# Spreading the weight statistics of a transformer layer: from one burst per attention head to pairs after each query tile, and into the output projection

## The reference

```python
x = x + attn(layernorm(x), Wq, bq, Wk, bk, Wv, bv, Wo, bo)   # causal, 16 heads of 128, rope
x = x + ffn(layernorm(x), w_gate, w_up, w_down)

def _weight_quant(w):
    scale = jnp.clip(jnp.mean(jnp.abs(w)), EPS, None)        # one number per matrix
    return jnp.clip(jnp.round(w / scale), -1.0, 1.0) * scale
def _bitlinear(x, w):
    return jnp.einsum('...i,oi->...o', _act_quant(x), _weight_quant(w))
# ffn: bitlinear(silu(bitlinear(x, w_gate)) * bitlinear(x, w_up), w_down)
```

## Time and profile before

| what | us |
|---|---|
| median of 13 runs (10388.69 to 10520.22) | 10472.44 |
| the profiled execution | 10480.55 |
| its span on the slowest core, core 4 | 10478.8 |
| spans of the eight cores | 10417.0 to 10478.8 |
| PE busy in the span | 6001.0 (57%) |
| DVE busy in the span | 4629.9 (44%) |
| ACT busy in the span | 1869.8 (18%) |
| POOL busy in the span | 1367.7 (13%) |

### The profile page before, as it was taken

How to read it: one execution, slowest core, us unless ns; L and a number is a source line. 1 busy time by engine, 2 the same in 40 slices (tenths; PEclk the granted TensorE clock), 3 DMA queues, 4 the chain that set the end, 5 groups by cost and what they waited for, 6 DMA issues and landing times.

```text
span 10478.8 us, 90777 instructions; the slowest of 8 cores (10417.0 to 10478.8 us)
## 1 busy us (share of the span) xinstructions
PE 6001.0 (57%) x23243; PEld 2279.6 (22%) x23698; DVE 4629.9 (44%) x5216; ACT 1869.8 (18%) x3294; POOL 1367.7 (13%) x770
## 2 busy tenths in 40 slices
PE   0007466596464545546455078788878826384847
PEld 0002222242010111101012033333333312232323
DVE  6403233223434334343436467777777642414140
ACT  3531011002232333323221000000000010101010
POOL 0002122000000000000000133333333200000000
PEclk9999799797676676767678589999999957686767
DMA  2482321331313132221344433343333213343323
GB/s 93 157 271 55 74 49 41 80 79 44 116 63 119 62 103 78 88 93 66 106 125 142 144 128 122 128 128 125 125 126 125 97 59 136 111 143 107 134 95 123
DMA packets 637659, 1115.47 MB, mean 106 GB/s; under 512 B 339954, under 2 KB 421874, under 8 KB 567282
## 3 DMA queue, kind: packets, MB, share of 16 engines
q1 hardware_dynamic: 433380, 530.71, 17.1%
q10 hardware_dynamic: 158976, 302.06, 8.3%
q0 software_dynamic: 44816, 276.88, 8.3%
HBM read 874.62 MB, written 218.10 MB: 104 GB/s over the span
## 4 chain that ended last, share of the span: by engine, by line
DVE 34%; PE 30%; DMA 10%; issue 7%; ACT 7%; POOL 5%; SPq 3%; ACTq 2%; DVEq 1%; another core or an unknown queue 1%; POOLq 0%
PE pb L68 23%; DVE p_cu L68 5%; PE p2S L68 3%; SPq L68 3%; DVE p_hqt L68 3%; DVE t_w L68 3%; DVE wa_tmp L68 2%; POOL p_wdtb L68 2%; DVE p_pm L68 2%; DVE p_wf L68 2%; ACTq L68 2%; ACT p_E L68 2%; DVE p_invr L68 2%; DMA wa_t<-wgT 2%; DMA wa_t<-wuT 2%
## 5 line engine op out<-in xcount | busy, mean ns | idle before, releaser
L68 PE MATMUL pb<-p_wgt,p_xiT 128*128 128x512 bf16 x4015 | 1073.1, 425 | 801.6 <-DVE p_ht L68 430.2
L68 PE MATMUL pb<-p_wds,p_hTg 128*128 128x512 bf16 x4009 | 1022.8, 422 | 104.8 <-DMA p_wds<-wdtd 88.5
L68 ACT ACTIVATE p_E<-pb,p_negB 128x512 bf16<-128x512 f32 x1280 | 879.4, 687 | 633.7 <-PE pb L68 452.4
L68 DVE TENSOR_TENSOR p_cu<-g_sxinv,p4a_swn 128x1 f32<-128x1 f32 x256 | 754.3, 2947 | 28.2 <-DVE p_cg L68 2.1
L68 PEld LDWEIGHTS pb<-p_wgt,p_xiT 128*128 128x128 bf16 x4096 | 426.9, 107 | 1431.0 <-issue 1072.5
L68 PE MATMUL p2S<-p_E,g_ones_colb 128*1 128x512 bf16 x1280 | 539.7, 422 | 308.4 <-DVE p_invr L68 307.0
L68 PE MATMUL pb<-k_pp_xT,k_pp_W 128*128 128x512 bf16 x2007 | 465.1, 383 | 299.7 <-ACT k_pp_qb L68 196.2
L68 PE MATMUL pb<-p_dump,g_ones_colb 128*1 128x512 bf16 x192 | 107.2, 593 | 910.5 <-DVE p_dump L68 791.5
L68 DVE TENSOR_REDUCE wa_tmp<-wa_t 128x1 f32<-128x2048 f32 x192 | 438.9, 2286 | 354.4 <-DMA wa_t<-wgT 120.0
L68 PEld LDWEIGHTS pb<-p_wds,p_hTg 128*128 128x128 bf16 x4096 | 433.4, 106 | 690.5 <-issue 501.6
L68 PE MATMUL pb<-p_qT,p_kT 128*128 128x512 bf16 x1263 | 551.5, 440 | 51.9 <-ACT p_E L68 38.9
(11 more groups left out here) (168 smaller groups left out, 6853.6 us busy)
## 6 DMA issues: line engine op xcount, KB each, us to landing
wa_t<-wgT POOLq DMA_DIRECT2D x64, 1024.0 KB, 5.9
wa_t<-wuT POOLq DMA_DIRECT2D x64, 1024.0 KB, 5.8
wa_t<-wdT POOLq DMA_DIRECT2D x64, 1024.0 KB, 5.4
p_wf<-wdT SPq DMA_DIRECT2D x64, 1024.0 KB, 5.9
p_wf<-wgT SPq DMA_DIRECT2D x64, 1024.0 KB, 5.8
p_wf<-wuT SPq DMA_DIRECT2D x64, 1024.0 KB, 5.3
hfpd<-p_ht ACTq DMA_DIRECT2D x256, 256.0 KB, 2.9
p_wds<-wdtd SPq DMA_DIRECT2D x64, 1024.0 KB, 6.5
```

The costliest lines, as they stand in the source:

```text
L68: real = getattr(eng, meth)(*a, **k)
```

## The change

The feed moves inside the loop over query tiles, with 2 chunks after each of the four tiles, in place of 12 after each head. That places 8 per head, 128 in attention. The other 64 go into the loop over row blocks of the output projection, 4 behind each block. The epilogue moves behind that loop.

```diff
@@ attention, loop over t @@
                 eitems.extend(mk_epi(h, t, t % 2))
+                wa_feed(2)
             hrel[sl] = (sT, sT.v)
-            wa_feed(12)
@@ output projection, ahead of the loop over tb @@
             wsem.inc(G.dma_start(dst3, rows), 16)
 
-        wa_feed(len(wa_items))
-        wa_epilogue()
         cin = [dm["c0"], dm["c1"]]
@@ end of the loop over tb @@
             x1rel[sl] = [(x1sem[sl], x1sem[sl].v), (sS, sS.v), (sV, sV.v)]
+            wa_feed(4)
+        wa_feed(len(wa_items))
+        wa_epilogue()
         wait(V, (sV, sV.v), (sS, sS.v))
```

## The result

The changed kernel took 10143.81 us in the median of 11 runs, the kernel before 10480.57 us in the median of 48. The ratio is 0.9672 (95% interval 0.9644 to 0.9701): 3.3% faster, some 337 us; the fastest runs of the two, 10382.44 and 10043.36 us, lie 339 us apart. The forecast was 10170 us.

What follows compares the result with a forecast made beforehand. DVE's chunk burst at each head's end was taken to bound attention, DVE the output projection's pace. From 10480.55 us, -728 +165 +23 +230 +8 gave 10179, less 8 for the median 10170; range 10,060 to 10,330.

Steps and rivals of the forecast that it cites:

- The burst leaves the head's end: Attention, head ends: PE's wait for the squares falls to 9.4 us per head over 14 heads, gaining 639.6 us.
- The tail of heads 14 and 15: Attention, last two heads: reciprocal waits of 51.7 and 51.4 us become ordinary tile ends of 7.3, gaining 88.5 us.
- Pairs behind the first three tiles: Attention, 48 tile ends: the pair delays the reciprocal, PE's wait grows from 3.84 to 7.3 us, costing 165 us.
- a sign of being wrong: Attention: the prediction counts as wrong if tile ends cost more than 8 us.
- The clock behind a longer wait: Attention, tile ends: longer idle keeps PE's clock low for longer, 1.5 us per head, costing 23 us in all.
- The upper bound of 71 us: Attention: cost of the clock term if all 48 longer gaps paid at the lower clock level.
- Four chunks in each row block: Output projection: each block grows by 14.4 us to 31.2, costing 230 us over 16 blocks.
- the epilogue's 8: Behind the output projection's loop: nothing covers the moved epilogue any more, costing 8 us.
- Wo's wait: Start of the output projection: PE's wait for Wo stays; two chunk loads issued behind Wo's parts add 0.
- Transfers did not bound the output projection: Denies a rival: output projection bound by transfers, blocks of 39 us, 125 us more, 10,295 us; chance 0.12.
- The head's load: Rival, head ends: k usable only with v, PE idles 23.6 us, 199 us more, 10,370 us; chance 0.06.
- The slower case: Rival, attention: the clock stays down throughout, 770 us more, 10,920 us; chance 0.04.

Runs made afterwards that it cites:

- e7: e6 with three slots for q, k and v, so a head's loads are issued a whole head earlier; 9,676 us, ratio 0.9217 to the kernel before.
- e4: The changed kernel with the pairs of the first three tiles one step later, behind the next tile's first reciprocal; ratio 0.9576 to the kernel before.
- e1: The changed kernel without any chunks, neither their loads nor their sums, epilogue still behind the output projection's loop; ratio 0.9295 to the kernel before.
- e8: The changed kernel with four chunk tiles in place of two, so a row block's four chunks are loaded ahead; ratio 0.9538 to the kernel before.
- e6: The changed kernel with all 192 chunks as pairs inside attention's tiles, none at tile ends or row blocks; 9,772 us, ratio 0.9320 to the kernel before.

## Why the prediction was right

**The burst leaves the head's end.** Forecast: 639.6 us less waiting for the squares, 9.4 us left per head. Measured: 648 less (791.5 to 143.4). Of the 143.4, the first two waits take about 20, as before, which leaves 8.8 per head. What came next was named rightly, k's landing, and e7 shows it by moving it away. The tail of heads 14 and 15, forecast at 88.5, can't be told apart from the next term in the sum of waits; their longest wait fell from 51.7 to 8.3, 1 us over the forecast.

**Pairs behind the first three tiles.** Forecast: +165 for 48 of them and -88.5 for the last two heads, so +76.5 on the reciprocal's waits. Measured: +77. Two of these 64 waits take 8.3 us, over the 8 us that the prediction set as a sign of being wrong; they are the ends of heads 14 and 15, and the median is 7.1. e4 shows that it was the order on DVE, not the work: the same pair behind the reciprocal costs next to none of it.

**The clock behind a longer wait.** This term of 23 us was mis-sized, its mechanism was right. On core 4 the first matmul of `p2S` behind the reciprocal took 0.38 us at 16 of 63 tile ends before, and at none after; the others took 0.58 or so the earlier trace rows. But few further key blocks are slow for it: of the 1280 matmuls of `p2S`, 274 took over 0.5 us before, 289 after and 279 in e1. Ten to fifteen key blocks at 0.63 us more each (1.48 less 0.85) would be 6 to 9 us, an estimate. It fits e1's 1 to 8 us, and the 4 to 6 us by which attention on cores 4 to 7 shortened less than the waits named above. The rule of the Trainium skill (TensorE: Matmul & The Clock Gate, section "Why this matters for your kernels") on idle gaps, which the prediction weighed, holds in its direction, since every gap now ends at the lower level. The upper bound of 71 us wasn't reached.

**Four chunks in each row block.** Forecast 230 us with the epilogue's 8 beside it, measured 244 on core 4. By e1 and e8 a block's price is 11.3 us of series work and 3.6 of waiting for loads, 14.9 against the forecast 14.4. The epilogue itself ran from 5384.2 to 5392.3, its 8 us; in e1, where it stands at the same place without chunks, the stage is 6 us over that of before. Wo's wait stayed at some 59 us from issue to first matmul (60.7 before), although the two chunk loads issued behind Wo needed up to 61.8 us to land: they came behind, as assumed.

**The rivals.** Transfers did not bound the output projection: blocks of 30.5 to 33.2 us, not 39, and e8 gained by putting more loads in flight. The head's load cost k's landing and no more. The slower case is out: attention's granted clock rose.

**The sum.** Attention: forecast -540, measured -563 on core 4. Output projection with the epilogue: +238 and +244. Net -302 and -319, and most of what lies between is the clock term. By the medians over the cores it is -588 and +245, net -343, and medians of whole runs differ by 337. Core 4, on whose rows the forecast was made, had the shortest attention of the eight before.

## What to carry to other kernels

Background work on an in-order engine cost what it delayed, not what it lasted: in attention of this kernel all 192 chunks cost 18 us between key blocks in which DVE is idle and 761 in bursts, and 128 of them cost 174 at tile ends ahead of a reciprocal. When a burst goes, ask which load it had hidden, and give that load an earlier issue too. A place off the former critical path is no free place: where the engine itself sets the pace, each chunk cost its full length here, and part of its load as well with only two tiles.

## What the runs showed of the hardware that was not expected

In eight of the ten profiled executions pairs of neighbouring cores lost some 20 to 120 us in one stage or two, and not always the same: cores 4 and 5 in the down projection of the kernel before (2050 and 2030 us against 1919 to 1938) and cores 2 and 3 in its attention (3006 and 3007 against 2929 to 2953), cores 4 and 5 in attention of e4 (2269 and 2262 against 2189 to 2214) and of e6 (2243 and 2239 against 2197 to 2208). These stretches (core 0 and core 4 of the kernel before, same code, the down projection, then two parts of it on core 4; columns as above) show it as clock:

```profile
8529.00:10448.00 1919.00, 1045.79 (x5120) 503.04 (x5120) 631.78 (x720) 245.36 (x1088) 130.41 (x128) 0.74 0.36 123
```

```profile
8429.00:10478.00 2049.00, 1147.93 (x5033) 528.95 (x5120) 631.17 (x719) 245.23 (x1088) 128.65 (x128) 0.69 0.33 115
...
9260.00:9292.00 32.00, 31.73 (x120) 13.28 (x122) 0.00 (x0) 0.00 (x0) 0.00 (x0) 0.81 0.34 112
9292.00:9324.00 32.00, 31.82 (x124) 13.38 (x125) 0.00 (x0) 0.00 (x0) 0.00 (x0) 0.81 0.21 79
```

The mean granted clock is 0.74 in the one and 0.69 in the other, and PE is busy for 102 us more. The last two rows show why: PE works almost without a break there, and the granted clock stands at 0.81. The matmuls take 0.434 to 0.438 us in these 64 us, 0.379 on core 0 from 9270 to 9290, where the granted clock is 1.00. So a granted clock between 0.50 and 1.00 is not always a mix of the two levels in time, as it was read ahead of the prediction. Added up over the clock's records in the trace, core 4 stood at 0.81 for 648 of the 2050 us and core 6 for none of its 1933. The other stages named above have 386 to 673 us of it on the cores that lost time. It costs only where PE's pace counts: cores 4 and 5 of e1 had some 1500 us of it in gate and up, and that stage is as long there as on the other cores (2558 and 2559 us against 2560 to 2563).

The profiled executions of the changed kernel and of e8 have no such stretch on any core, and every core of e4's has over 1500 us of it. The rows on which the prediction and the account of it rest hold none: attention on core 4 before, and the changed kernel. What sets it off is open. It is why steps of 1% are read from stages and waits here rather than from the total.
